# A transposed set-up of the chunk's triangular system, with 16-column merges

## What is computed

```python
q = l2norm(q) * DK ** (-0.5)
k = l2norm(k)
def step(S, inp):
    qt, kt, vt, gt, bt = inp
    S = S * jnp.exp(gt)[..., None, None]
    v_new = vt - jnp.einsum('bhk,bhkv->bhv', kt, S)
    S = S + bt[..., None, None] * (kt[..., :, None] * v_new[..., None, :])
    o = jnp.einsum('bhk,bhkv->bhv', qt, S)
    return (S, o)
```

## Time and profile before

| what | value |
|---|---|
| runs, median (lowest to highest) | 422.68 us (421.88 to 423.92) |
| profiled execution | 424.54 us |
| its span, first to last instruction | 422.7 us |
| mean granted TensorE clock | 0.766 of full |
| VectorE, TensorE, ScalarE, GpSimd busy | 315.2, 268.4, 142.2, 45.8 us |

### The profile page before, as it was taken

One profiled execution on the slowest core, in us unless ns is written; L12 is line 12 of the kernel. 1 busy time (PEld: TensorE's weight loads), 2 busy tenths in 40 slices (PEclk: granted clock), 3 DMA queues, 4 the chain that ended last, 5 costly groups with the idle time before them and its releaser, 6 DMA issues.

```text
span 422.7 us, 14141 instructions
## 1 busy us (share of the span) xinstructions
PE 268.4 (63%) x6314; PEld 181.3 (43%) x6314; DVE 315.2 (75%) x790; ACT 142.2 (34%) x341; POOL 45.8 (11%) x59
## 2 busy tenths in 40 slices
PE   3992710598576639797586559785666093986552
PEld 1481500545454417364554436454534072754431
DVE  0765998938698993949698996767989938248996
ACT  0874540047704610354523412357036000232010
POOL 1000240002520000012320000025200000000000
PEclk9965675589867867988666679897888567899665
DMA  8400000000000010000000020000000111000101
GB/s 255 181 0 2 2 0 0 5 2 3 4 3 2 4 50 3 2 3 2 3 4 2 3 99 3 2 4 2 5 2 2 51 51 53 3 3 14 40 0 50
DMA packets 8012, 9.70 MB, mean 23 GB/s; under 512 B 1808, under 2 KB 7056, under 8 KB 7952
## 3 DMA queue, kind: packets, MB, share of 16 engines
q1 hardware_dynamic: 7024, 8.41, 6.0%
q10 hardware_dynamic: 928, 0.39, 0.4%
HBM read 6.70 MB, written 2.10 MB: 21 GB/s over the span
## 4 chain that ended last, share of the span: by engine, by line
DVE 53%; PE 30%; issue 7%; ACT 6%; DMA 1%; DVEq 0%; SPq 0%; ACTq 0%
PE pc L333 7%; PE pj L346 6%; PE pg L457 4%; DVE sub_buf L1027 3%; DVE conv_buf L928 3%; DVE sub_buf L1025 3%; PE fr L572 2%; PE fr L480 2%; PE pj L457 2%; PE fr L333 2%; DVE chunk_buf L984 2%; DVE r_sb L1073 2%; DVE ss L962 2%; DVE r_all L916 1%; DVE t_all L915 1%
## 5 line engine op out<-in xcount | busy, mean ns | idle before, releaser
L928 DVE SCALAR_TENSOR_TENSOR conv_buf<-raw,wconv,conv_buf 128x512 f32<-128x512 f32 x72 | 55.5, 777 | 16.5 <-ACT conv_buf L624 14.8
L346 PE MATMUL pj<-xt,wproj 128*128 128x512 f32 x96 | 54.6, 705 | 8.2 <-DMA xt<-x_t 7.3
L686 ACT ACTIVATE u_sb<-pc 128x192 f32<-128x192 f32 x32 | 10.5, 329 | 116.3 <-PE pc L333 116.2
L876 POOL TENSOR_TENSOR s_dec<-s_sb,decay 128x192 f32<-128x192 f32 x24 | 14.5, 602 | 264.2 <-DVE s_sb L1082 169.6
L333 PE MATMUL pc<-r_sb,t_t 32*32 32x64 f32 x672 | 17.8, 244 | 35.2 <-DVE r_sb L1073 34.5
L333 PEld LDWEIGHTS pc<-r_sb,t_t 32*32 32x32 f32 x672 | 12.6, 120 | 46.0 <-DVE r_sb L1073 42.8
L333 PE MATMUL fr<-dt_m,chunk_buf 32*32 32x32 f32 x768 | 10.5, 219 | 34.3 <-DVE dt_m L1041 20.2
L346 PEld LDWEIGHTS pj<-xt,wproj 128*128 128x128 f32 x96 | 19.4, 221 | 26.9 <-issue 22.6
L358 PE MATMUL pg<-xt,wproj 128*128 128x512 f32 x48 | 29.6, 747 | 0.0
L457 PE MATMUL pg<-wout,conv_buf 128*128 128x256 f32 x36 | 15.2, 607 | 19.5 <-DVE conv_buf L1119 19.5
L333 PEld LDWEIGHTS fr<-dt_m,chunk_buf 32*32 32x32 f32 x768 | 9.7, 131 | 35.9 <-issue 35.9
(11 more groups left out here) (161 smaller groups left out, 577.4 us busy)
## 6 DMA issues: line engine op xcount, KB each, us to landing
xt<-x_t SPq DMA_DIRECT2D x1, 1536.0 KB, 9.1
x_buf<-x SPq DMA_DIRECT2D x3, 512.0 KB, 3.8
out<-hid_buf SPq DMA_DIRECT2D x6, 256.0 KB, 2.2
wproj<-w_proj SPq DMA_DIRECT2D x1, 1024.0 KB, 8.1
xt<-x_t SPq DMA_DIRECT2D x1, 512.0 KB, 5.9
kq<-x SPq DMA_DIRECT2D x1, 512.0 KB, 3.7
out<-v_tok SPq DMA_DIRECT2D x2, 256.0 KB, 2.1
wout<-w_out SPq DMA_DIRECT2D x1, 384.0 KB, 9.5
```

The costliest lines, as they stand in the source:

```text
L346: mm = pe.matmul(pj[:, j % 2, :], wproj[:, t, j * P:(j + 1) * P], xt[:, t, k * TOK:(k + 1) * TOK], start=(t == 0), stop=(t == KT - 1))
L686: act.activation(u_sb[:, :, :].rearrange("p g v -> p (g v)"), pc[:, 0:G3 * DV], ACT.Copy).then_inc(u_done, 1)
L876: pool.tensor_tensor(s_dec[:, :, :], s_sb[:, :, :], decay[:, :, c:c + 1].to_broadcast([P, G3, DV]), ALU.mult).then_inc(sdec_done, 1)
L928: e = dve.scalar_tensor_tensor(out=conv[:, d, :, :], in0=raw[:, d, :, m:m + T], scalar=wconv[:, j, m:m + 1], in1=conv[:, d, :, :], op0=ALU ...
```

## The change

VectorE computes 1/|k|^2 by a reciprocal ahead of the square root, forms c2 from it, and multiplies c2 into the decay matrix itself, in place. The factor then belongs to the column side: the system is set up transposed (x_m, upper triangular), so neither the decay matrix nor the off-diagonal block is transposed, and the key's norm is multiplied onto the inverse (`inverse`: norm, norm_a). The values go into the scan unscaled, so `v_scaled` and rv go and v_tok has two buffers. GpSimd loses `c_masked` and `k_decayed`; the latter's product moves to VectorE (kg_tok in `scaled_operands`). The upper right block goes to x12 by one ScalarE instruction (`upper_right`) at chunk 5. Both merges have 16 columns a unit, for all 24 units at once and before the second part of `project_out`. Cut to its core (the removed lines stand in the code above):

```diff
-v_tok = sb("v_tok", [P, G3, NC, 2, DV // 2])
+v_tok = sb("v_tok", [P, 2, G3, NC, 2, DV // 2])
...
-d_m = view(chunk_buf, 0, U, CH)
...
+x_m = view(chunk_buf, 0, U, CH)
 a_t = sb("a_t", [P, 2, U, CH])
 l16 = sb("l16", [P, HALF, CH])
-l21 = sb("l21", [P, U, CH])
...
+x12 = sb("x12", [P, U, CH])
+inv16 = sb("inv16", [P, HALF + 1, CH + 1])
+x16 = sb("x16", [P, CH, HALF])
+x16_t = sb("x16_t", [P, CH, HALF])
+prod16 = view(sub_buf, 0, (HALF // 2) * HALF)
...
     def merge(k):
-        after(pe, l21_done, 1, k, 1)
-        after(pe, x32_done, 1, k, 1)
+        after(pe, x12_done, 1, k, 1)
+        after(pe, x16_done, 1, k, 2)
         after(pe, at_done, 1, k, 1)
-        for n in range(2):
...
+        for u in range(U):
+            mm = by_head(fr[:, 0, u * HALF:(u + 1) * HALF], x12[:, u, :], x16_t[:, u, :],
+                         start=True, stop=True)
+        mm.then_inc(p_mm, 1)
+    def merge_second(k):
+        after(pe, x16_done, 2, k, 2)
+        after(pe, p_done, 1, k, 1)
+        for u in range(U):
+            mm = by_head(fr[:, 2, u * HALF:(u + 1) * HALF], p_sb[:, u, :], x16[:, u, :],
+                         start=True, stop=True)
         mm.then_inc(merge_mm, 1)
...
-            after(pe, tt_done, 2, k, 2)
-            after(pe, rv_done, 1, k, 1)
+            after(pe, tt_done, 1, k, 1)
+            after(pe, v_tok_done, 1, k, 1)
...
             mm = by_head(pc[:, g * DV:(g + 1) * DV], t_t[:, g * NC + c, :],
-                         rv[:, k % 2, g, 0, :] if c == 0 else r_sb[:, g, :], start=True, stop=True)
+                         v_tok[:, k % 2, g, 0, :, :].rearrange("p h v -> p (h v)") if c == 0 else r_sb[:, g, :], start=True, stop=True)
         mm.then_inc(u_mm, 1)
...
-        merge_second(k, 0)
+        merge_second(k)
         if tail:
             project_out(k - 1, 1)
-        merge_second(k, 1)
...
+    def upper_right(k):
+        after(act, x_done, 1, k, 1)
+        if not first(k):
+            after(act, p_mm, 0, k, 1)
+        act.activation(x12[:, :, HALF:CH], x_m[:, :, HALF:CH], ACT.Identity,
+                       scale=cst[:, C_ROWA:C_ROWA + 1]).then_inc(x12_done, 1)
     def merge_out(k):
         if not first(k):
-            after(act, merge_mm, 0, k, 2)
...
+            after(act, merge_mm, 0, k, 1)
+        after(act, p_mm, 1, k, 1)
+        act.activation(p_sb[:, :, 0:HALF], fr[:, 0, 0:U * HALF].rearrange("p (u t) -> p u t", u=U),
+                       ACT.Copy).then_inc(p_done, 1)
...
-    def v_scaled(k, chunks):
...
-        for c in chunks:
...
                 exp_d(k + 1)
                 silu(k + 1, 5)
-            if front and c >= 5:
-                v_scaled(k + 1, ((0, 1, 2), (3, 4, 5), (6, 7))[c - 5])
+            if front and c == 5:
+                upper_right(k + 1)
...
-    act.wait_ge(zeroed, 1)
+    act.wait_ge(zeroed, 4)
...
     pool.memset(raw[:, :, :, 0:TAPS - 1], 0.0).then_inc(zeroed, 1)
-    pool.memset(l21[:, :, :], 0.0).then_inc(zeroed, 1)
+    pool.memset(x12[:, :, :], 0.0).then_inc(zeroed, 1)
+    pool.memset(p_sb[:, :, :], 0.0).then_inc(zeroed, 1)
...
     def g_masked(k):
         after(pool, park_done, 1, k, 1)
         if not first(k):
-            after(pool, tt_done, 0, k, 2)
+            after(pool, dt_done, 0, k, 1)
         pool.tensor_tensor(gm[:, :, :], units(park[:, 0, :]), upper, ALU.mult).then_inc(gm_done, 1)
     def d_masked(k):
         after(pool, dexp_done, 1, k, 1)
+        if not first(k):
+            after(pool, at_done, 0, k, 1)
         pool.tensor_tensor(dt_m[:, :, :], dexp[:, :, :], upper, ALU.mult).then_inc(dt_done, 1)
-
...
     def v_to_tokens(k):
         after(dve, silu_done, CONV_TILES, k, CONV_TILES)
-        if not first(k):
-            after(dve, rv_done, 0, k, 1)
+        if k > 1:
+            after(dve, u_mm, 0, k - 1, NC)
         for h in range(2):
-            e = dve.transpose(v_tok[:, :, :, h, :], v_ch[:, :, h, :].rearrange("p g (c t) -> p g c t", c=NC))
+            e = dve.transpose(v_tok[:, k % 2, :, :, h, :], v_ch[:, :, h, :].rearrange("p g (c t) -> p g c t", c=NC))
...
         kk3 = kk[:, :].rearrange("p (g c) -> p g c", g=G3)
         own(dve.tensor_scalar(kk3, ss[:, :, 0, :], EPS_K, None, ALU.add))
+        own(dve.reciprocal(rt[:, :], kk[:, :]))
+        own(dve.scalar_tensor_tensor(out=c2[:, :], in0=rt[:, :], scalar=0.5, in1=park[:, 1, :],
+                                     op0=ALU.mult, op1=ALU.mult))
+        dve.tensor_tensor(fg[:, :], c2[:, :], park[:, 3, :], ALU.mult).then_inc(c2_done, 1)
         rsqrt(r2[:, :], kk[:, :], rt[:, :])
-        own(dve.tensor_tensor(rt[:, :], r2[:, :], r2[:, :], ALU.mult))
+        own(dve.scalar_tensor_tensor(out=fk[:, :], in0=r2[:, :], scalar=-1.0, in1=park[:, 2, :],
+                                     op0=ALU.mult, op1=ALU.mult))
+        own(dve.tensor_tensor(norm[:, :], r2[:, :], kk[:, :], ALU.mult))
+        own(dve.tensor_scalar(norm_a[:, :], norm[:, :], cst[:, C_ROWA:C_ROWA + 1], None, ALU.mult))
+    def scaled_operands(k):
+        def tokens(v):
+            return v.rearrange("p (g c) d -> p g c d", g=G3)
+        def rows(v):
+            return v.rearrange("p (g c) -> p g c", g=G3).unsqueeze(3).to_broadcast([P, G3, NC, DK])
         if not first(k):
-            after(dve, cm_done, 0, k, 1)
...
+            after(dve, x12_done, 0, k, 1)
+        dve.tensor_tensor(tokens(kc_tok), kq_tok[:, :, 0, :, :], rows(fk[:, :]), ALU.mult).then_inc(kc_part, 1)
+        dve.tensor_tensor(tokens(qe_tok), kq_tok[:, :, 1, :, :], rows(park[:, 2, :]),
+                          ALU.mult).then_inc(kc_part, 1)
         if k > 1:
+            after(dve, s_mm, 0, k - 1, NC - 1)
             after(dve, o_mm, 0, k - 1, NC)
+        dve.tensor_tensor(tokens(kg_tok[:, k % 2, :, :]), kq_tok[:, :, 0, :, :], rows(fg[:, :]),
+                          ALU.mult).then_inc(kg_done, 1)
+        after(dve, kc_part, 1, k, 2)
         dve.transpose(kc_ch[:, k % 2, :, :].rearrange("p u t -> p (u t)"),
-                      kc_tok[:, :, :].rearrange("p u t -> p (u t)")).then_inc(kc_done, 1)
+                      kc_tok.rearrange("p u t -> p (u t)")).then_inc(kc_done, 1)
+        after(dve, kc_part, 2, k, 2)
         dve.transpose(qe_ch[:, k % 2, :, :].rearrange("p u t -> p (u t)"),
-                      qe_tok[:, :, :].rearrange("p u t -> p (u t)")).then_inc(qe_done, 1)
+                      qe_tok.rearrange("p u t -> p (u t)")).then_inc(qe_done, 1)
     def chunk_matrices(k):
         after(dve, dt_done, 1, k, 1)
+        own(dve.tensor_tensor(dt_m[:, :, :], dt_m[:, :, :],
+                              c2[:, :].unsqueeze(2).to_broadcast([P, U, CH]), ALU.mult))
         after(dve, kc_done, 1, k, 1)
-        own(dve.transpose(d_m[:, :, :].rearrange("p u t -> p (u t)"),
-                          dt_m[:, :, :].rearrange("p u t -> p (u t)")))
         after(dve, ga_mm, G3, k, G3)
         prod = fr[:, :, :].rearrange("p g (c k t) -> p (g c) k t", c=NC, k=2)
-        own(dve.tensor_tensor(gd[:, :, :], prod[:, :, 0, :], d_m[:, :, :], ALU.mult))
-        if k > 1:
-            after(dve, o_mm, 0, k - 1, NC)
+        dve.tensor_tensor(x_m, prod[:, :, 0, :], dt_m[:, :, :], ALU.mult).then_inc(x_done, 1)
         dve.tensor_tensor(a_t[:, k % 2, :, :], prod[:, :, 1, :], dt_m[:, :, :], ALU.mult).then_inc(at_done, 1)
-        after(dve, cm_done, 1, k, 1)
...
+        after(dve, x_done, 1, k, 1)
+        own(dve.scalar_tensor_tensor(out=l16[:, :, 0:U].rearrange("p t u -> p u t"), in0=x_m[:, :, HALF:CH],
+                                     scalar=cst[:, C_LESS_B:C_LESS_B + 1], in1=x_m[:, :, 0:HALF],
                                      op0=ALU.mult, op1=ALU.subtract))
-        own(dve.tensor_scalar(l21[:, :, 0:HALF], lo[:, :, 0:HALF], row_b, None, ALU.mult))
...
+        after(dve, qe_done, 1, k, 1)
+        own(dve.transpose(columns[:, :, :, :].rearrange("p c h i -> p (c h i)"),
                           l16[:, :, :].rearrange("p t u -> p (t u)")))
+        own(dve.memset(diagonal, 1.0))
+    flat = inv16[:, :, :].rearrange("p c i -> p (c i)")
+    columns = flat[:, 0:HALF * CH].rearrange("p (c h i) -> p c h i", c=HALF, h=2)
+    diagonal = inv16[:, 0:HALF, 0:HALF + 1:HALF]
     def substitute(j):
         rows = HALF - 1 - j
-        grid = [P, j, 2, rows]
...
+        grid = [P, rows, 2, j]
+        step = prod16[:, 0:2 * j * rows].rearrange("p (c h i) -> p c h i", c=rows, h=2)
+        right = columns[:, j + 1:HALF, :, 0:j]
+        own(dve.tensor_tensor(step, columns[:, j:j + 1, :, 0:j].to_broadcast(grid),
+                              columns[:, j + 1:HALF, :, j:j + 1].to_broadcast(grid), ALU.mult))
+        own(dve.tensor_tensor(right, right, step, ALU.add))
+    def inverse_to_rows(k):
         if not first(k):
-            after(dve, merge_mm, 0, k, 2)
...
+            after(dve, merge_mm, 0, k, 1)
+        dve.transpose(x16_t[:, :, :].rearrange("p u i -> p i u"),
+                      columns[:, :, :, :].rearrange("p c h i -> p i h c")).then_inc(x16_done, 1)
```

(19 more changed lines are left out.)

151 lines of the change are left out of this document (22 added, 129 removed).

## The result

The changed kernel takes **408.79 us** (median of 4 runs, 408.38 to 410.49) beside 423.24 us (421.88 to 423.92) of the kernel before: a ratio of 0.967, interval 0.963 to 0.971. Measured once more beside another set of runs of the kernel before (424.58 us), the same program took 408.81 us. The forecast was 409.0 us. It was counted down by 13.7 us from 422.68 us; beside the runs of the same series the gain is 14.5 us, and 15.8 us in the second series. The profiled execution took 409.17 us, its span 407.3 us.

A forecast was written before the change was run, and what follows sets the result against it. VectorE's own order was taken to bound the kernel. Prologue with turn 0 -3.4, three turns -10.5, handoffs -0.3 and collision +0.5 sum to -13.7 us, from 422.68 to 409.0 us; range 402.8 to 414.5.

The forecast's parts named there:

- Step 1: Factors block of each set-up: new tiny VectorE instructions, a reciprocal among them, replace four; +0.64 us per set-up.
- Step 2: Scaled operands of each set-up: three VectorE products of 768 elements replace six of 256; -0.74 us a turn, -1.2 in the prologue.
- Step 3: Chunk matrices of each set-up: two transpositions and two products go, one product and a memset come; -2.24 us.
- Step 4: Substitution in each set-up: same 28 instructions of the same sizes, two inner dimensions swapped; 0 us.
- Step 5: End of each set-up: two strided transpositions of 512 elements, taken at 1.2 us each, replace the old work; -1.15 us.
- A: Rival: set-up transpositions at the packed price and the state of chunk 6 at its early end; 403.5 us, chance 0.18.
- C: Rival: the transpositions ending each set-up cost 1.8 us each; 413.8 us, chance 0.11.
- Step 6: Scan beside the set-ups: state wait 0 on balance (-0.5 to +0.1), o_square covered; turn 0's longer inverse +0.54 us.
- Step 7: Handoffs of turns 1 to 3: all 192 merge products ahead of the second projection; -0.1 us each, -0.3 in all.
- Step 8: Turn 2: GpSimd's decay mask newly collides with VectorE's taps of tile 5; 0 to +0.9 us, +0.5 taken.
- Rival B: Front turns: the scan, not VectorE, ends them, a turn gaining 2.1 and not 3.5 us; 413.2 us, chance 0.14.
- D: Rival: TensorE's granted clock falls, making the kernel slower than before; 429 us at clock 0.66, chance 0.04.

The follow-up runs named there:

- the second execution: The changed kernel executed once more without any edit, showing what one execution scatters; the repeat of the changed kernel took 408.81 us.

## Why the prediction was right

The mechanism was right: the set-ups are VectorE's own time, and they shrank by the work that went. The 0.2 us between forecast and median flatter it. The profiled execution came out 1.6 us from its forecast (409.17 for 410.8), the gain within one series is 14.5 or 15.8 us where 13.7 was forecast, and several terms were off by more and cancelled. The set-ups gave 17.9 us where 14.4 were forecast (3.95 and three times 3.49) and the handoffs 2.0 more than their 0.3; turn 0 took 1.2 more back, the collision 0.6 more, and 2.0 came in stretches that the change doesn't touch. That these fell out to so little is luck.

- **Step 1**: +0.71 for +0.64. The reciprocal of 24 elements takes 0.30 us, 0.34 from its start to the next one's, where 0.30 was taken for that. In the prologue norm_a stood under GpSimd's mask for 1.86 us; the block came one instruction earlier than I had placed it (I had the first scaled product held back). Factors and scaled operands of pair 0 together gained 0.1 us and not 0.56 (11.73 for 11.82), as an instruction of 24 elements was held up in place of one of 768 with its 0.9 us of work; the end of that set-up gained 1.64 and not 1.15. The sum, -3.96 for -3.95, is two misses that cancelled.
- **Step 2**: -0.81 for -0.74. **Step 3**: -2.26 for -2.24; the terms as listed add up to 4.68 and not 4.6, so to -2.14, and the memset of the diagonal took 0.12 us to the next start and not 0.20. These are sums of durations of equal instructions and held to about 0.1 us.
- **Step 4**: 0, as seen.
- **Step 5**: the transpositions, besides the reciprocal the one price without a row, were taken at 1.2 us and measured 1.05 and 1.00, so -1.45 in turn 1 and -1.64 to -1.68 in the other set-ups for -1.15. A's 0.71 and C's 1.8 are both refuted. The estimate from strided products was right in kind and in rate: 512 elements at its 0.7 to 0.8 ns are 0.36 to 0.41 us more (I made 0.4 to 0.5 of it), 1.07 to 1.12 in all, and 1.2 was taken above that. What it had open, whether two strided sides cost twice, came out as once. The Trainium skill (Vector Engine (DVE) Microarchitecture Reference, section 3.8) has the transposing front-end sustain one element per cycle per lane; read as the price of every access pattern, which the section doesn't say, that would have kept all at the packed price. The trace shows 0.67 to 0.71 us only where input and output are both packed.
- **Step 6**: this is the term that was mis-sized most. I set the state of chunk 6 at "0 on balance, -0.5 to +0.1"; VectorE's wait for it fell from 1.01 or 1.02 to 0.32 us in every turn (0.42 in turn 0 of the second execution), outside that range. This half of rival A did come. The time of r was right: 216.15 is 222.70 on the clock of the trace before, where 222.72 was forecast. That of TensorE's second gate product was not: it was to be over 0.64 later, just behind r, and was over 0.25 earlier, at 215.84, 0.3 ahead of r; the granted clock of the scaled operands' stretch had risen from 0.50 to 0.63. The second thing left out is the clock behind the wait: TensorE waits 0.72 us and not 2.84, and its two steps take 0.54 us each and not 0.86. From the start of r to the state 2.06 us pass, where 2.72 passed, and that is nearly the whole of the gain. The run with two more transpositions turned exactly this back in turns 0 and 1, and not in turn 2, where TensorE waited 2.75 us and kept the higher level: that VectorE's shorter work can bring the gain is shown, what sets the level is not. With step 5's gain the turns gained 4.70, 4.49 and 4.72 us and not 3.49.
- **Step 6, turn 0**: +0.54 was taken for the longer inverse and +1.7 measured (+2.3 in the second execution). VectorE waits 0.87 us for the second merge, where before its taps lasted until the merge was over; TensorE's merges in the prologue run at a granted clock of 0.50 in both kernels, and TensorE stands still inside them twice, for 1.72 and 1.69 us (1.51 and 1.62 before), with no wait that the profile shows:

```profile
81.22 1.26 PE L329 MATMUL fr<-x,p_sb 32*32 32x16 f32 x79 [1.69 <-issue]
82.61 0.61 DVE L1013 SCALAR_TENSOR_TENSOR t_t<-x,cst,fr 128x384 f32<-128x384 f32 x1 [0.87 <-PE fr L329]
```

  Its first solve starts 1.0 us earlier than before although the set-up ended 2.6 us earlier by the clock of the two traces. The merges had been hidden and came onto the path: the term that I had left out. Why TensorE stops there is open.
- **Step 7**: 192 merge products in 1.79 us, where I took 1.7 between 1.02 and 2.04. The handoffs moved by -0.87, +0.02 and -1.44 us and in the second execution by -0.5, +0.2 and -0.7, not by the -0.1 that was looked for. Most of it is the first output projection's clock: 5.49, 4.27 and 5.49 us before (granted clock 0.50, 0.66, 0.50), 4.84, 4.28 and 4.28 after. That this is scatter and not the change is borne out by the kernel before with its c2 product on VectorE, whose handoffs take 12.16, 11.91 and 11.77 us, 2.1 us less than in the profiled execution of the kernel before.
- **Step 8**: the collision came where it was foreseen, but larger than its range (0 to +0.9) and in one turn more: the taps of tile 5 take 3.87 us and not 2.68, +1.2, in turns 1 and 2 alike. In turn 1 it isn't seen in the stretch (38.69 for 38.75) because TensorE's four products for the exponents ran there in 1.56 us and not in 2.89. The row that gave the upper bound had another mask beside the taps. The Trainium skill (SBUF — State Buffer, Who interferes with whom) has a VectorE instruction with two SBUF inputs contend with a GpSimd one that reads SBUF, for an exclusive lock. Its price, near 0.9 by my reckoning, was the nearer one, and still 0.3 short; GpSimd's mask grew too, from 1.81 to 2.24 us. The 24-element instruction that took 1.47 us beside the 1.48 of GpSimd's is a tensor_scalar with one tensor input and not of that pair: the same section lets a tensor_scalar block GpSimd only in a two-port mode, and no view here shows the mode.

Rival B did not come: o_square was ready before VectorE wanted it even with ScalarE's copies brought back. D did not either: the mean granted clock rose from 0.766 to 0.792. The account of the profiled executions: set-ups -17.9, rest of the prologue and turn 0 +1.7, turn 2's collision +1.1, handoffs -2.3, the start +1.35 and turn 3 +0.65 (neither in the forecast), turn 1's middle and the gating stretches -0.1: -15.5, as the end of VectorE's last instruction moved (420.13 to 404.66).

## What to carry to other kernels

Where one engine is busy back to back in a stretch, add up the durations of equal instructions and trust the sum; spend the doubt on the operations that no row shows and on what was hidden behind the part that shrinks. Check a total that fits term by term: here two misses of 0.5 us cancelled in the prologue alone. Read every GpSimd product against what VectorE does at that moment, even an instruction of 24 elements, and move either of the two. Halving the columns of the merge products from 32 to 16 bought nothing here, as their count stayed.

## What was not expected of the hardware

- A VectorE tensor_scalar of 24 elements took 1.86 us beside a GpSimd product of 1.80 us, and 1.47 us beside one of 1.48, against 0.24 alone and 0.17 for its neighbour: in both cases the block was as long as GpSimd's product, however short the instruction.
- A 32-by-32 block transposition of 512 elements per partition costs 0.67 to 0.71 us packed and 1.00 to 1.05 with a stride on input, output or both.
- 32-row TensorE products cost some 9 ns each with 16 and with 32 columns (192 in 1.79 and 1.82 us, at the higher clock).
- The same TensorE steps took 0.54 us behind a wait of 0.72 and 0.86 behind one of 2.62 or 2.84 us, but 0.54 again behind one of 2.75; behind one of 1.39 us and one short step four projection instructions took 3.31 and not 1.96. Work taken off another engine can so pay twice, when TensorE's steps behind the shorter wait run at the higher clock; a longer wait does not always lose it.
- TensorE stood still for 1.7 us twice inside a run of merge products of the prologue, and for 2.04 us once in another kernel's handoff, with no wait that the profile shows. No run here tells why.
